# Edge attention on one core: two weight halves ahead of the held-back product sums, exp sums of two blocks in the message stage

## What is computed

```
def _L1_gnn_ref(feat, efeat, W_msg, b_msg, W_attn, b_attn, src, dst):
    w_m = (efeat @ W_msg + b_msg).reshape(E, in_f, -1)      # 16 x 16 a edge
    w_a = (efeat @ W_attn + b_attn).reshape(E, in_f, -1)
    h_src = feat[src][:, :, None]
    e1 = w_m * h_src
    e2 = w_a * h_src
    seg_max = jax.ops.segment_max(e2, dst, num_segments=N)
    ex = jnp.exp(e2 - seg_max[dst])
    denom = jax.ops.segment_sum(ex, dst, num_segments=N)
    attn = ex / denom[dst]
    ft = jax.ops.segment_sum(e1 * attn, dst, num_segments=N)
    return ft.sum(axis=1)
```

## Time and the profile before

| | us |
|---|---|
| median of 3 runs | 5954.85 (5950.09 to 5958.16) |
| the profiled execution, its own time | 5951.75 |
| its span in the trace | 5949.9 |
| VectorE busy | 3470.4 |
| TensorE busy (matmul) | 2723.7 |
| GpSimd busy | 4176.8 |
| ScalarE busy | 1369.4 |

### The profile page before, as it was taken

One profiled execution on the slowest core, in us unless ns is written; L12 is line 12 of the kernel. 1 busy time (PEld: TensorE's weight loads), 2 busy tenths in 40 slices (PEclk: granted clock), 3 DMA queues, 4 the chain that ended last, 5 costly groups with the idle time before them and its releaser, 6 DMA issues.

```text
span 5949.9 us, 57446 instructions
## 1 busy us (share of the span) xinstructions
PE 2723.7 (46%) x13577; PEld 1930.7 (32%) x13578; DVE 3470.4 (58%) x4171; ACT 1369.4 (23%) x1709; POOL 4176.8 (70%) x3713
## 2 busy tenths in 40 slices
PE   2550000000000000000668888788888888878887
PEld 1110000000000000000446666565656565655565
DVE  8601222222222223332688888888888888888886
ACT  2540000000000000010223232333333333333333
POOL 2237777777777777765477878777777777777763
PEclk9999999999999999999978888888889888988998
DMA  4881111111111111110111111111111111111110
GB/s 145 285 264 27 29 22 28 29 30 35 29 29 36 29 36 36 36 34 19 21 22 22 22 24 28 22 22 30 22 22 30 22 30 22 30 22 30 30 30 19
DMA packets 157959, 251.69 MB, mean 42 GB/s; under 512 B 73726, under 2 KB 130563, under 8 KB 145156
## 3 DMA queue, kind: packets, MB, share of 16 engines
q0 software_dynamic: 126192, 100.10, 9.4%
q1 hardware_dynamic: 31711, 151.31, 7.7%
q10 hardware_dynamic: 32, 0.01, 0.0%
HBM read 113.57 MB, written 136.63 MB: 42 GB/s over the span
## 4 chain that ended last, share of the span: by engine, by line
POOL 28%; PE 23%; issue 15%; DVEq 14%; DVE 12%; DMA 5%; POOLq 1%; ACT 1%; SPq 0%; ACTq 0%
POOL gath L359 26%; PE psS L568 10%; PE psS L573 8%; DVEq L1228 7%; DVE stage L1187 4%; DMA table<-arena 4%; PE psW L562 3%; DVE stage L1231 3%; DVEq L1194 2%; DVEq L1187 1%; DVEq L1156 1%; PE psW L516 1%; DVEq L1143 1%; ACT arena L650 1%; DVE arena L1187 1%
## 5 line engine op out<-in xcount | busy, mean ns | idle before, releaser
L359 POOL DMA_INDIRECT gath<-h_dram,hidx x1695 | 2119.4, 1250 | 732.2 <-issue 556.0
L359 POOL DMA_INDIRECT gath<-table,blkidx x1646 | 1639.6, 996 | 508.2 <-issue 505.0
L556 PE MATMUL psT<-identb,stage 128*100 128x128 bf16 x2448 | 226.2, 251 | 2340.2 <-DVEq L1143 2321.9
L573 PE MATMUL psS<-stage,ident 128*128 128x256 f32 x3390 | 930.1, 430 | 169.6 <-DVE stage L1231 169.1
L556 PEld LDWEIGHTS psT<-identb,stage 128*100 128x100 bf16 x2448 | 201.6, 150 | 2380.7 <-DVEq L1143 2279.7
L568 PE MATMUL psS<-arena,ident 128*128 128x256 f32 x3390 | 823.8, 380 | 0.2 <-issue 0.2
L573 PEld LDWEIGHTS psS<-stage,ident 128*128 128x128 f32 x3390 | 705.3, 216 | 322.0 <-DVE stage L1231 212.4
L787 DVE TENSOR_TENSOR work<-gath 128x768 f32<-128x768 f32 x50 | 48.2, 965 | 1284.9 <-DMA gath<-table,blkidx 1284.9
L1187 DVE TENSOR_TENSOR arena<-psW,gath 128x768 f32 (+1 forms) x565 | 523.7, 952 | 438.0 <-PE psW L562 301.5
L562 PE MATMUL psW<-wst,stage 100*128 100x256 bf16 x3390 | 574.5, 290 | 241.6 <-DVE arena L1187 164.9
L717 ACT ACTIVATE arena<-arena 128x1536 f32<-128x1536 f32 (+1 forms) x294 | 421.4, 1433 | 894.4 <-DVE arena L1218 894.4
(11 more groups left out here) (227 smaller groups left out, 2395.4 us busy)
## 6 DMA issues: line engine op xcount, KB each, us to landing
table<-arena SPq DMA_DIRECT2D x50, 1610.0 KB
ef<-arena SPq DMA_DIRECT2D x50, 805.7 KB
gath<-h_dram,hidx POOLq DMA_INDIRECT x1695, 2.4
gath<-table,blkidx POOLq DMA_INDIRECT x1646, 2.4
arena<-in_edge_attr SPq DMA_DIRECT2D x50, 257.8 KB
table<-arena SPq DMA_DIRECT2D x50, 186.9 KB
arena<-first_dram POOLq DMA_DIRECT2D x1, 915.5 KB, 12.3
info<-info_dram POOLq DMA_DIRECT2D x2, 432.0 KB, 10.4
```

Of the source, the lines that this page charges most:

```text
L359: pool.indirect_dma_start(out=gath[:, q, s, :], out_offset=None, in_=rows, in_offset=bass.IndirectOffsetOnAxis(ap=idx[:, q, s:s + 1].bitca ...
L556: last = nc.tensor.transpose(psTb[0:KE, t % 2, j, 0:GP], efs[:, 8 * t + j, :], identb[0:GP, 0:GP])
L573: nc.tensor.matmul(psS[0:GP, IO:2 * IO], ident[0:GP, 0:GP], prod[:, c0:c0 + IO], start=False, stop=False)
```

## The change

In the score stage the first two halves have no weights step any more: TensorE makes the weights of halves 0 and 1 of the next window at the end of the message stage, before it waits for the last block. The product sums of a window's last block (`last_sums`) are held back to the start of the next window's program; as their place in the ring depends on the window, their addresses are computed in registers. The exp sums of the first four halves (OWN = 2 blocks) are made in the message stage of their own window, each block's behind its product sums; those of the other halves stay in the score stage of the next window.

```
+OWN = 2
-            def prod_sums(h):
-                for s in range(HALF):
-                    c0 = (h % (2 * RING) * HALF + s) * IO
-                    nc.tensor.matmul(psS[0:GP, IO:2 * IO], ident[0:GP, 0:GP], prod[:, c0:c0 + IO], start=False, stop=False)
+            def prod_sums(base):
+                for j in range(HALF):
+                    nc.tensor.matmul(psS[0:GP, IO:2 * IO], ident[0:GP, 0:GP], prod[:, ds(base + j * IO, IO)], start=False, stop=False)
+
+            def ring_free():
+                nc.tensor.matmul(psS[0:GP, IO:2 * IO], zero[:, 0:GP], zero[:, 0:IO], start=False,
+                                 stop=False).then_inc(m["q_free"], 1)
+
+            def last_sums(nh, done):
+                pe.wait_ge(m["q_ready"], done)
+                base = (blocks(nh) + (RING - 1)) % RING * (BLK * IO)
+                prod_sums(base)
+                with pe.If(nh % 2 < 1):
+                    prod_sums(base + HALF * IO)
+                ring_free()
...
+            pe.wait_ge(m["efT_sb"], S // 8 + 2)
+            for h in range(2):
+                weights(0, 0, h, 0)
             with pe.Fori(0, pairs) as i:
...
-                    pe.wait_ge(m["efT_sb"], k * (S // 8) + (S // 8 + 2))
-
-                    for h in range(NHW):
+                    with pe.If(prev > 0):
+                        last_sums(prev, tb)
+                    for h in range(2, NHW):
                         if h < MINH:
                             weights(0, q, h, tb * 4)
                         else:
                             with pe.If(nh > h):
                                 weights(0, q, h, tb * 4)
-                        with pe.If(prev > h):
-                            exp_sums(1 - q, h)
+                        if h >= 2 * OWN:
+                            with pe.If(prev > h):
+                                exp_sums(1 - q, h)
...
-                        with pe.If(nb > b):
+                        if b < OWN:
                             pe.wait_ge(m["q_ready"], tb + (b + 1))
-                            prod_sums(2 * b)
-                            with pe.If(nh > 2 * b + 1):
-                                prod_sums(2 * b + 1)
-                            nc.tensor.matmul(psS[0:GP, IO:2 * IO], zero[:, 0:GP], zero[:, 0:IO], start=False,
-                                             stop=False).then_inc(m["q_free"], 1)
+                            for h in range(2):
+                                prod_sums((2 * b + h) * HALF * IO)
+                            ring_free()
+                            for h in range(2):
+                                exp_sums(q, 2 * b + h)
+                        elif b < NBW - 1:
+                            with pe.If(nb > b + 1):
+                                pe.wait_ge(m["q_ready"], tb + (b + 1))
+                                for h in range(2):
+                                    prod_sums((2 * (b % RING) + h) * HALF * IO)
+                                ring_free()
+                    pe.wait_ge(m["efT_sb"], k * (S // 8) + (2 * (S // 8) + 2))
+                    for h in range(2):
+                        weights(0, 1 - q, h, tb * 4 + nb * 4)
                     pe.reg_add(cumb, cumb, nb)
                     pe.reg_mov(nhp, nh)
             prev = pe.snap(nhp)
-            for h in range(NHW):
+            last_sums(prev, pe.snap(cumb))
+            for h in range(2 * OWN, NHW):
                 with pe.If(prev > h):
                     exp_sums(1, h)
             close_sums()
```

## The result

The changed kernel takes 5918.52 us (median of 4 runs, 5915.98 to 5922.92), the kernel before 5956.51 us (4 runs, 5950.09 to 5960.44). The ratio is 0.9938, 95% interval 0.9925 to 0.9952: faster by 38 us, where 95 were forecast. 5918.5 lies in the range given, 5790 to 5935, but outside the forecast's own, 5835 to 5890. Ratios are to the kernel before on the same chip, from undisturbed runs.

The account below looks back on a forecast made before the run. VectorE was taken to bound the second layer, waiting 273.8 us for score weights. Saving 200, less 95 for message waits and 10 for GpSimd, gives 95: 5954.85 to 5860 us, own range 5835 to 5890, wide range 5790 to 5935.

Parts of the forecast that it names:

- G: VectorE's wait for weights before a window's first score half, 4.07 us on average; predicted to vanish.
- three 0.67s: VectorE's waits of 0.67 us before each of score halves 1, 2 and 3; predicted to go.
- Remaining: 73 us: Score-stage waits left over 45 windows: 21 odd at 1.0, 14 long at 1.5, 10 short at 3.1 us.
- 2.65 us: Time taken for the last block's held-back product sums at the window's end, from 2.86 less an overlap.
- ends at 4476.58 + 0.99 = 4477.57, before L1231's end, and costs nothing: Early weights' wait for the last feature copy in windows of twelve halves, put at no cost.
- Cost 1.8 to 2.4 us a window, I take 2.1: 95 us: New VectorE waits for weights in the message stage, caused by the moved exp sums of blocks 0 and 1.
- Block 3: Message-stage wait before block 3: TensorE needs 6.6 us, VectorE 5.25, so 1.35 us more.
- Block 2: Message-stage wait before block 2: 0.4 us, or 1.0 where the first product sums took 4.50.
- GpSimd, -10 us: Deduction of 10 us from the saving for gathers not keeping up in windows of 13 and 14 halves.
- the band that I had given to GpSimd: Rival: GpSimd becomes the bound as gathers meet more of L1231; some 50 us gained, 5890 to 5935, chance 0.19.
- Low clock of the moved exp sums: Rival: message-stage exp sums take 5.2 us, not 2.6; 117 us more, 5977; chance 0.10 with other losses.
- held-back sums ... take over 4 us: Sign that the forecast is wrong: held-back sums with computed addresses taking over 4 us.

Follow-up runs that it names:

- the copies' repair: The changed kernel, but the two early weights halves wait for the first feature copy only, the full wait coming before half 2: 5896.1 us, ratio 0.9891.
- the order alone: The kernel before with early weights and held-back product sums, but all exp sums in the next window's score stage: 5920.38 us, ratio 0.9928.
- kept-busy kernel: The changed kernel with sixteen zero matmuls filling TensorE's idle pieces around the early weights in even windows: 6011.53 us, ratio 1.0081; on two slower chips 1.024 and 1.0216.
- both repairs: The changed kernel with one half's exp sums at each of four blocks and early weights behind the first copy only: 5823.65 us; on slower chips 6293.49 and 6295.78.

## Why the prediction was off

By its own steps:

- **G goes, and one wait before half 2 takes the place of three 0.67s**: right in kind. G was predicted away, "bound is below by 0"; what stands in its place is 0.85 to 1.31 us before the first half in 40 of the windows, at VectorE's own loop instructions or for the weights, and 2.0 to 2.3 in five. That it doesn't matter up to 1.5 was right in windows of 14 halves: 0.85 + 1.19 there and 1.30 + 0.74 in the next both make 2.04.
- **"Remaining: 73 us"**: this is the term that failed most, by 44 us. It measured 117.6. The 14 windows that end with 14 or 12 message halves wait 49 us (3.3 of it for gathers) against 21 worked out, the ten of 10 or 8 halves 36 against 31, the 21 odd ones 32 against 21.
  In the windows of twelve halves the step that failed is the product sums' "2.65 us", which is the high clock. Eight of the ten sets take 4.51 us, and these windows wait 4.2 us each where the two with a fast set wait 2.2: 15 of the 44 us. Most of the rest in the long windows is that the sums start 0.35 to 0.9 us behind L1257's end, where the sum had 0.1. I had charged the low clock to the ten short windows by half, where no set is slow; they wait because the early weights and so the sums come late. Of the odd windows three of the six with 13 halves wait 2.8 us, and in the one looked at (held-back set at 3570.72) the block before has its twelve passes at 4.54 us; the others wait 1.1 to 1.7. To the long windows I had charged no low clock, since there the copy "ends at 4476.58 + 0.99 = 4477.57, before L1231's end, and costs nothing". In the timeline above TensorE waits 1.14 us for that copy (ACT L733), then another 1.07, and the passes are at 0.68 and 0.59 of the clock:

```profile
4480.20:4482.60 2.40, 2.35 (x8) 1.96 (x9) 1.82 (x2) 1.47 (x7) 1.79 (x3) 0.68 0.60 239
4482.60:4484.90 2.30, 2.30 (x7) 1.42 (x5) 0.00 (x0) 0.06 (x1) 1.09 (x2) 0.59 0.05 7
```

  The granted clock is 1.00 in the 9.2 us ahead of this. The copy did end (4478.16) before L1257 (4479.33), but TensorE stood idle for it. That the slower passes are the price of this is not shown: the copies' repair gave 18.5 us back and leaves four slow sets of ten, the filled pieces leave ten of ten, and at the end of a window of 14 halves a set takes 2.83 us behind an idle piece of 1.64 (3218.73).
- **"Cost 1.8 to 2.4 us a window, I take 2.1: 95 us"**: 110 measured, 2.44 a window. Block 3 is exact (1.35 worked out, 1.40 in the row). Block 2 is at 1.0, the upper end of the 0.4 to 1.0 worked out: the first product sums take 4.3 us on average, 4.63 in the window where the earlier trace rows has 3.91.
- **GpSimd, -10 us**: 3.3 us of waits for gathers are there, and with a third of the gathers the 45 windows are the same. The term wasn't needed. The row that spoke for the rival, a gather of 2.45 us beside L1231, is right as a row, but the gathers did not meet more of them: in the 45 windows their mean is 1.26 us before, 1.21 in the changed kernel and 1.29 with the order alone. So GpSimd's idle pieces beyond the regular 0.30 did not fall to half, as forecast; they went from 172 to 192 us, although the windows got shorter.
- **Sum**: 156 - 110 = 46 us in the windows, 200 - 95 - 10 = 95 predicted. The first two terms are off by 44 and 15, the third by 10 the other way: 49. The rest to the measured 38 lies ahead of the second layer, where the changed kernel's profiled execution came 12 us later to L1224 than the one before to L1198. The edit touches nothing there; its relatives lie between 4 and 16 us above the one profiled execution of before, and the unchanged kernel's second one had its first gather 8.9 us later too. So most of it is scatter; a second trace of the kernel before on a chip of the same kind, which would show it for L1198, is missing.
- **The rivals**: the measured time falls in the band that I had given to GpSimd, 5890 to 5935, and the cause is not GpSimd: same place, wrong reason. That the time lies in the range at all is owed to a band drawn for another cause. "Low clock of the moved exp sums" is wrong, they run in 2.86 us; the low clock hit the product sums ahead of them and those at the window's end. The sign "held-back sums ... take over 4 us" did show, in eight sets of 25.

What I had not seen at all is that on top of the new order leaving the exp sums in the score stage costs as much as moving them in lumps does: a wait before half 3, `finish` waiting for sums that close later, and waits for gathers, which take 1.29 us each there and not 1.21, are 86 of the 107 us together. That these gather waits go when gathers are taken away is shown by a run; the other two are read from the waits. The clock's part is small and not of one sign, as the windows of ten and of twelve halves show. No run changes the clock by itself, and the one that tried missed.

Open stay: why the gathers are slower with the order alone; why the passes behind idle pieces of about 1 us are slow in eight of the ten windows of twelve halves and fast in two; why the kept-busy kernel, with two skipped conditionals more, stands still for 5 us and more in some odd windows; and what "remote" is on the two chips where the kernel before takes 6277 us.

## What to carry to other kernels

When work is moved from one engine's critical stage into the slack of another, look at the slack piece by piece: 2.6 us in two blocks that have 1.3 us of room each costs 110 us, and the same passes at 1.3 us in four blocks cost 22 and make the kernel 94 us faster. Cost a chain on TensorE at both clock levels whenever it comes behind an idle piece: eight of 25 sets took 4.5 us in place of 2.8. When work is left where it is or put back, ask also what stands behind it, here the closing of the sums. And measure the two parts of a change alone before believing a sum over them: here -41 and +41 gave about -41.

## What the runs showed of the hardware

- Twelve passes of the same shape took 2.8, 4.5 or 5.5 us at a granted clock of 1.00, 0.62 and 0.50 over their time; 0.50 is the level of 1.2 GHz throughout, and 0.62 is that level for most of it. They took 4.51 us behind idle pieces of 1.14 and 1.07 us, and 2.83 us behind one of 1.64.
- With sixteen zero matmuls of one partition in the place of 2 us of idle time the clock was at 0.63 and the passes took 4.51 us all the same.
- TensorE's standstills of 5.4 to 6.9 us, in every second window of eleven halves, came with two skipped conditionals more in its loop; no run shows these to be the cause.
- The kernel before takes 5957 to 5965 us in three comparisons and 6277 to 6280 us in two others, on two other chips. VectorE's standstills that the profile puts down to "remote" are up to 4.0 us long there in its 45 windows, and up to 16.5 us in the kernel with both repairs. With a third of the gathers there are none in the 45 windows, and one of up to 79.5 us ahead of them.
